# Causal attention block on one core: a power and a few idle products moved, and the mask of the narrow diagonal tiles added by TensorE

## Chip, cores and metric

One core of a Trainium2 chip runs the whole kernel. The metric is the device time of one execution in microseconds (us). The kernel before was timed three times.

## What is computed

One transformer layer over 8 sequences of 1024 tokens with 256 channels, 16 heads of 16 channels, in fp32:

```
mod = (silu(c) @ wmod) in six parts sa, ca, ga, sb, cb, gb
h = layernorm(x) * (1 + ca) + sa
scores = q @ k^T * 16 ** -0.5, the future keys masked; att = softmax(scores) @ v
x = x + ga * (att @ w_out + b_out)
h = layernorm(x) * (1 + cb) + sb
r = sigmoid(mix(h, mu_r) @ W_r); k = relu(mix(h, mu_k) @ W_k) ** 2
out = x + gb * r * (k @ W_v)
```

`mix(h, mu)` is `mu * h + (1 - mu) * (h shifted by one token)`. Full precision of the dense products comes from three products of split operands (hi by hi, hi by lo, lo by hi).

## The kernel before

Every engine has its program written out by hand; semaphores tie them. A sequence b is cut into four quarters s of four heads, a quarter into 12 steps t. In a quarter three things run side by side.

**Columns.** For the heads of quarter s, `score_columns` (L1246) makes scores with the keys on the partitions, in two PSUM banks `col_ps`. ScalarE takes the exponential into `weights` (`exps`, L823). In steps 0 to 3 and 8 to 11 the tile has the diagonal in it and GpSimd zeroes the future keys (`select`, L669). `values` (L1309) multiplies the weights of the step before with v. Steps 0 to 3 and 8 to 11 have 512, 384, 256 and 128 queries a head, steps 4 to 7 have 512.

**Rows.** The exponential needs the maximum of each query over its keys beforehand. So while quarter s runs its columns, `row_pair` (L1287) makes the scores of quarter s+1 with the queries on the partitions, in four banks `row_ps`, and VectorE reduces each bank to a maximum (`maximum`). A row unit is one bank: for query tile i, keys up to 512 or the rest. A diagonal unit ends at the diagonal. With up to 256 keys a unit holds two heads, otherwise one. A quarter has 40 units, handed out to steps by `PER_STEP`, two by two, those of even heads and odd heads on the two halves of the array's rows. The first two of a step are its early units, the others its late ones. In a diagonal unit `maximum` runs one fused add-and-max per head with `row_mask` (L1044, a CUSTOM_DVE instruction and one that reads its accumulator). In another unit it runs one TENSOR_REDUCE (L1048). A bank can be written again once its maximum has been taken (`row_bank`).

The narrow diagonal units are those of two heads: i = 0 (128 keys a head) early in step 0, i = 1 (256 keys) late in step 0, the second part of i = 4 (128) early in step 4, the second part of i = 5 (256) early in step 6. Each stands for a pair of banks: four pairs a quarter, 128 pairs in the run.

**Dense units.** Between them run the products of the next sequence (q, k, v and transposes, `front`) and of the sequence that has left attention (`back`: out, norm, recept, key, value, at steps 2, 6, 10, 11 and 13 of a quarter's own count, so that 12 to 15 fall into the next quarter). The recept and key products wait for `mix_lo` (L725), the value product for `k_lo` (L729), both made by GpSimd. In quarter 0 VectorE takes the layernorm sums of the next sequence (`layernorm_stats`, steps `STATS_STEPS`, L1082 and L1086), and GpSimd turns them into reciprocal deviations with a power (`rstd`, steps `RSTD_STEPS`, L655 to L660). ScalarE uses them in steps 2 and 3 of quarter 1. GpSimd's program in a step is: front, back, select, rstd, finish.

**Unused products.** `keep_load` (L1261) makes eight products of 512 columns into two `col_ps` banks that nobody reads, in quarters 2 and 3 at the start of step 3 and in quarters 1 and 3 at the columns of step 4. They first wait until the exponentials have left the banks.

TensorE's order in a step is: early rows, columns, values of the step before, then late rows and second columns (late rows first where a dense unit follows), dense units.

## Time and profile before

| | |
|---|---|
| median of 3 runs | 1496.95 us (1493.8 to 1501.97) |
| the profiled execution | 1493.7 us, its span 1492.0 us |
| mean granted TensorE clock | 0.961 of full speed |
| busy | TensorE 1339.4, its weight loads 759.3, VectorE 1153.5, ScalarE 958.3, GpSimd 666.9 us |

The profile comes from one execution. A row of the timeline gives the start, the duration of the merged group, the engine, the line, the operation and, in brackets, the idle time before it with what ended it. PE is TensorE's products, PEld its weight loads, DVE VectorE, ACT ScalarE, POOL GpSimd. Times in brackets are what a step of the chain waited; a matmul's duration holds its way through the array, so that the spacing of starts tells what a product takes from the stream.

### The profile page before, as it was taken

The numbers are of one execution on the slowest core, as the hardware profiler recorded it, in microseconds if no ns is written. First come the engines' busy times: TensorE is split into PE (matmuls) and PEld (weight loads), VectorE is DVE, ScalarE is ACT, GpSimd is POOL, SyncE is SP. The second block draws the span as 40 slices with busy tenths as digits, with TensorE's granted clock in tenths as the row PEclk, the third lists the DMA queues.
The fourth block names the chain that finished last, engine by engine and source line by source line (L and its number), as shares of the span: only waits on it lengthen the run. The fifth ranks groups of instructions, "written<-read, shape, count | busy, mean of one in ns | idle before, by whom it ended". The sixth has DMA issues, their size and how long they took to land.

```text
span 1492.0 us, 28255 instructions
## 1 busy us (share of the span) xinstructions
PE 1339.4 (90%) x9000; PEld 759.3 (51%) x9000; DVE 1153.5 (77%) x3627; ACT 958.3 (64%) x1916; POOL 666.9 (45%) x1042
## 2 busy tenths in 40 slices
PE   5799988999989999899999999899999999999855
PEld 4444444455644556555554556445555555544444
DVE  8788878877778778887788777787788777888234
ACT  2067666766668666667667666686666676666634
POOL 4023123544445444553445445454445535444554
PEclk9599999999999999999999999999999999999978
DMA  4322233212331224222332123312232222321100
GB/s 142 61 68 53 55 77 89 58 52 73 102 81 45 54 67 113 65 55 66 76 93 59 52 72 102 81 46 54 74 109 62 55 66 74 97 63 52 38 30 29
DMA packets 84133, 102.84 MB, mean 69 GB/s; under 512 B 20736, under 2 KB 49672, under 8 KB 83984
## 3 DMA queue, kind: packets, MB, share of 16 engines
q1 hardware_dynamic: 83408, 100.24, 25.4%
q8 instruction: 72, 1.18, 0.3%
q10 hardware_dynamic: 576, 0.79, 0.3%
q14 instruction: 77, 0.63, 0.1%
HBM read 31.74 MB, written 8.94 MB: 27 GB/s over the span
## 4 chain that ended last, share of the span: by engine, by line
PE 64%; ACT 12%; POOL 7%; issue 7%; DVE 6%; SPq 2%; DMA 2%; ACTq 0%; POOLq 0%; DVEq 0%
PE val_ps L1309 15%; PE col_ps L1246 14%; PE row_ps L1287 11%; ACT weights L823 7%; PE dense_ps L1347 5%; PE dense_ps L1319 4%; PE dense_ps L1321 3%; PE dense_ps L1320 3%; POOL weights L669 3%; PE dense_ps L1362 2%; PE dense_ps L1353 2%; SPq L498 2%; PE col_ps L1261 2%; PE dense_ps L1338 1%; ACT xn_c L867 1%
## 5 line engine op out<-in xcount | busy, mean ns | idle before, releaser
L823 ACT ACTIVATE weights<-col_ps 128x512 f32<-128x512 f32 (+2 forms) x1280 | 643.8, 556 | 285.5 <-PE col_ps L1246 270.1
L1044 DVE CUSTOM_DVE_ANT_0 row_ps<-row_ps,row_mask 128x128 f32<-128x128 f32 (+3 forms) x1024 | 477.2, 518 | 172.5 <-PE row_ps L1287 169.8
L669 POOL TENSOR_SCALAR_AFFINE_SELECT weights<-weights 128x256 f32<-128x256 f32 x512 | 211.3, 422 | 524.8 <-ACT weights L823 521.3
L1246 PE MATMUL col_ps<-q_stack,k_stack 64*128 64x512 f32 (+3 forms) x1536 | 394.1, 392 | 24.5 <-ACT weights L823 21.5
L1048 DVE TENSOR_REDUCE max_parts<-row_ps 128x1 f32<-128x512 f32 x512 | 328.1, 682 | 58.9 <-PE row_ps L1287 57.4
L1287 PE MATMUL row_ps<-k_stack,q_stack 62*128 62x512 f32 (+3 forms) x1536 | 328.4, 419 | 25.4 <-DVE max_parts L1048 10.9
L1309 PE MATMUL val_ps<-weights,v_ones 128*32 128x512 f32 (+3 forms) x3072 | 333.4, 506 | 18.1 <-POOL weights L669 9.2
L1246 PEld LDWEIGHTS col_ps<-q_stack,k_stack 64*128 64x128 f32 x1536 | 205.4, 187 | 209.0 <-ACT weights L823 191.5
L1287 PEld LDWEIGHTS row_ps<-k_stack,q_stack 62*128 62x128 f32 x1536 | 158.5, 190 | 226.4 <-DVE max_parts L1044 73.5
L1044 DVE DVE_READ_ACCUMULATOR2_ANT max_parts<- 128x1 f32 x1024 | 145.0, 142 | 0.0
L1309 PEld LDWEIGHTS val_ps<-weights,v_ones 128*32 128x32 f32 x3072 | 61.5, 108 | 105.2 <-issue 59.8
L725 POOL TENSOR_TENSOR mix_lo<-mixed,mix_hi 128x512 fp32r<-128x512 f32 x64 | 81.3, 1293 | 17.4 <-ACT mix_hi L916 15.2
L718 POOL TENSOR_TENSOR h_diff<-h 128x512 f32<-128x512 f32 x32 | 33.3, 1041 | 109.1 <-ACT h L887 108.9
L1148 DVE SCALAR_TENSOR_TENSOR mixed<-h_diff,mus,h 128x256 f32<-128x256 f32 x128 | 63.3, 535 | 10.2 <-POOL h_diff L718 10.2
L1319 PE MATMUL dense_ps<-h_hi,w_hi 128*128 128x512 f32 x124 | 55.5, 448 | 3.2 <-POOL h_lo L644 3.2
L1076 DVE STREAM_TRANSPOSE max_rows<-max_parts 32x32 f32<-32x32 f32 x256 | 51.3, 200 | 5.1 <-DVE max_parts L1070 0.3
L897 ACT ACTIVATE h_diff<-dense_ps 128x512 f32<-128x512 f32 x28 | 16.7, 598 | 57.1 <-PE dense_ps L1368 57.1
L1321 PE MATMUL dense_ps<-h_hi,w_lo 128*128 128x512 f32 x124 | 49.2, 397 | 0.0
L1320 PE MATMUL dense_ps<-h_lo,w_hi 128*128 128x512 f32 x124 | 49.0, 395 | 0.0
L894 ACT ACTIVATE mix_out<-dense_ps 128x512 f32<-128x512 f32 x28 | 16.8, 598 | 49.1 <-PE dense_ps L1353 49.1
L679 POOL TENSOR_TENSOR h_lo<-h_full,h_hi 128x512 fp32r<-128x512 f32 x28 | 35.9, 1280 | 26.7 <-DVE h_full L1108 26.7
L729 POOL TENSOR_TENSOR k_lo<-k_sq,k_hi 128x512 fp32r<-128x512 f32 x28 | 36.3, 1295 | 21.5 <-ACT k_hi L921 21.5
(196 smaller groups left out, 1946.0 us busy)
## 6 DMA issues: line engine op xcount, KB each, us to landing
q_stack<-q_part SPq DMA_DIRECT2D x384, 64.0 KB, 2.2
k_stack<-k_part SPq DMA_DIRECT2D x372, 64.0 KB, 2.2
xa<-in_x SPq DMA_DIRECT2D x9, 1024.0 KB, 6.4
att<-val_out SPq DMA_DIRECT2D x64, 128.0 KB
recips<-recip_rows SPq DMA_DIRECT2D x32, 256.0 KB
xq<-in_x SPq DMA_DIRECT2D x28, 256.0 KB, 3.2
out<-xq SPq DMA_DIRECT2D x28, 256.0 KB, 2.1
q_stack<-max_rows SPq DMA_DIRECT2D x128, 8.0 KB
```

The costliest lines, as they stand in the source:

```text
L669: nc.gpsimd.affine_select(out=w, in_=w, compare_op=ALU.is_ge, fill=0.0, base=0, pattern=[[0, 2], [1, P]], channel_multiplier=-1).then_inc( ...
L725: nc.gpsimd.tensor_tensor(mix_lo[:, m], mixed[:, m], mix_hi[:, m].bitcast(F32), ALU.subtract).then_inc(mix_lo_done, 1)
L823: nc.scalar.activation(weights[:, t % 2, heads[0]:heads[-1] + 1:2, 0:q1 - q0], col_ps[bank][:, 0:n * (q1 - q0)].rearrange("p (h q) -> p h ...
L1044: last = nc.vector.tensor_tensor_reduce(out=scores, in0=scores, in1=row_mask[:, HALF - width:HALF], scale=1.0, scalar=MASKED, op0=ALU.add, ...
L1048: last = nc.vector.reduce_max(dest, bank[:, 0:len(heads) * width].rearrange("p (h k) -> p h k", h=len(heads)), AX_X)
L1246: last = nc.tensor.matmul(col_ps[bank][:, i * (q1 - q0):(i + 1) * (q1 - q0)], stack_at(k_stack[s % 2], rows, heads[i], P * j, P * (j + 1)) ...
L1287: last = nc.tensor.matmul(banks[odd][:, n * width:(n + 1) * width], stack_at(q_stack[stack], rows, heads[n], P * i, P * (i + 1)), stack_at ...
L1309: last = nc.tensor.matmul(val_ps[32 * h:32 * h + 32, q0 - base:q1 - base], v_ones[:, j, G * s + h].rearrange("p d a -> p (d a)"), weights[ ...
L1319: nc.tensor.matmul(dst, a_hi(c), b_hi(c), start=(c == 0), stop=False)
L1320: nc.tensor.matmul(dst, a_hi(c), b_lo(c), start=False, stop=False)
L1321: last = nc.tensor.matmul(dst, a_lo(c), b_hi(c), start=False, stop=(c == KC - 1))
L1347: nc.tensor.matmul(dense[:, i, :], a_hi[:, c, P * i:P * (i + 1)], w(part, at, D)(c), start=(part is w_hi and i == 0 and c == 0), stop=Fals ...
```

## The change

Three things. (1) `RSTD_STEPS` goes from (0, 9) and (1, 0) to (0, 8) and (0, 11), and the last of `STATS_STEPS` from 11 to 9. (2) The unused products of quarters 2 and 3 at the start of step 3 go behind the values of step 3, ahead of its late rows, and take the banks of step 4, so that they wait for the exponentials of step 3. (3) In narrow diagonal units TensorE adds the mask: per head and half two products of `mask_ident` (64 rows by 128, bf16, an identity in two pieces) with `mask_fill` (bf16, -3e38 above the diagonal), 128 and 64 columns wide, accumulated onto the scores. VectorE then runs one TENSOR_REDUCE over both heads. Wide diagonal units (one head a bank) stay as they were. The constants are built by GpSimd at the start.

```
-LOAD_AT_START, LOAD_AT_COLUMNS, LOADS = ((2, 3), (3, 3)), ((1, 4), (3, 4)), 4
-SPLIT_STEP, STATS_STEPS, NORM_STEPS = 5, (5, 7, 8, 11), (2, 2, 3, 3)
-RSTD_STEPS = ((0, 9), (1, 0))
+LOAD_AT_ROWS, LOAD_AT_COLUMNS, LOADS = ((2, 3), (3, 3)), ((1, 4), (3, 4)), 4
+SPLIT_STEP, STATS_STEPS, NORM_STEPS = 5, (5, 7, 8, 9), (2, 2, 3, 3)
+RSTD_STEPS = ((0, 8), (0, 11))
...
 # maximum, VectorE
-                if k1 == P * (i + 1):
-                    for n in range(len(heads)):
-                        scores = bank[:, n * width:(n + 1) * width]
-                        last = nc.vector.tensor_tensor_reduce(...)
+                if k1 == P * (i + 1) and len(heads) == 1:
+                    scores = bank[:, 0:k1 - k0]
+                    last = nc.vector.tensor_tensor_reduce(...)
                 else:
                     last = nc.vector.reduce_max(...)
...
 # keep_load(b, s, t, after), TensorE
-                            pe.wait_ge(exp_done, exp_index(b, s, COL_FIRST[t] + odd) + (1 - ago))
+                            pe.wait_ge(exp_done, exp_index(b, s, COL_FIRST[t + after] + odd) + (1 - ago))
...
 # row_pair, TensorE
+                diagonal = k1 == P * (i + 1) and len(pair[0]) == 2
-                        end = n == len(heads) - 1
+                        end = n == len(heads) - 1 and not diagonal
...
+                for n in range(len(pair[0])) if diagonal else ():
+                    for a in range(2):
+                        for odd in range(2):
+                            rows = slice(ROW_TILE * odd, ROW_TILE * (odd + 1))
+                            end = n == len(pair[0]) - 1 and a == 1
+                            last = nc.tensor.matmul(banks[odd][:, (n + 1) * width - P + ROW_TILE * a:(n + 1) * width],
+                                                    mask_ident[rows, a, :], mask_fill[rows, a, ROW_TILE * a:P],
+                                                    start=False, stop=end, skip_group_check=True)
+                            if end:
+                                last.then_inc(rows_ready, 1)
...
 # body, TensorE
-                    if (s, t) in LOAD_AT_START and attends(kind):
-                        keep_load(b, s, t)
                     row_scores(b, s, early)
...
                     for c in cols[1:]:
                         score_columns(b, s, t, c)
+                    if (s, t) in LOAD_AT_ROWS and attends(kind):
+                        keep_load(b, s, t, 1)
                     if not dense_step:
                         row_scores(b, s, late)
```

GpSimd in quarters 0 and 1 of a sequence, from step 8 of quarter 0 (`h_diff` is made there) to step 1 of quarter 1. Before:

```order
L718 TENSOR_TENSOR h_diff<-h_0 128x512
L669 AFFINE_SELECT weights<-weights 128x2x128 x4
L655 TENSOR_SCALAR shift_a<-mv_a 128x4
L656 TENSOR_SCALAR var_a<-mv_a 128x4
L658 TENSOR_TENSOR rstd_a<-var_a,neg_half 128x4
L660 TENSOR_TENSOR shift_a<-shift_a,rstd_a 128x4
L725 TENSOR_TENSOR mix_lo<-mixed,mix_hi 128x512 x2
L669 AFFINE_SELECT weights<-weights 128x2x128 x6
L655 TENSOR_SCALAR shift_a<-mv_a 128x4
L656 TENSOR_SCALAR var_a<-mv_a 128x4
L658 TENSOR_TENSOR rstd_a<-var_a,neg_half 128x4
L660 TENSOR_TENSOR shift_a<-shift_a,rstd_a 128x4
```

`k_lo` follows. The same place in the change, from behind `h_diff` on:

```order
L682 AFFINE_SELECT weights<-weights 128x2x128 x2
L668 TENSOR_SCALAR shift_a<-mv_a 128x4
L669 TENSOR_SCALAR var_a<-mv_a 128x4
L671 TENSOR_TENSOR rstd_a<-var_a,neg_half 128x4
L673 TENSOR_TENSOR shift_a<-shift_a,rstd_a 128x4
L682 AFFINE_SELECT weights<-weights 128x2x128 x2
L738 TENSOR_TENSOR mix_lo<-mixed,mix_hi 128x512 x2
L682 AFFINE_SELECT weights<-weights 128x2x128 x4
L668 TENSOR_SCALAR shift_a<-mv_a 128x4
L669 TENSOR_SCALAR var_a<-mv_a 128x4
L671 TENSOR_TENSOR rstd_a<-var_a,neg_half 128x4
L673 TENSOR_TENSOR shift_a<-shift_a,rstd_a 128x4
```

The first power goes from ahead of `mix_lo` to ahead of the two selects of step 9, the second from behind the selects of the next quarter's step 0 to ahead of them; `k_lo` then follows those selects.

TensorE in quarter 2, steps 3 and 4, around the eight unused products (L1261 before, L1271 in the change). Before, from the unused products on:

```order
L1261 MATMUL col_ps1<-q_stack0,k_stack0 128x512
L1287 MATMUL row_ps0<-k_stack1,q_stack1 128x512
L1287 MATMUL row_ps1<-k_stack1,q_stack1 128x512
...
L1309 MATMUL val_ps<-weights,v_ones 32x256 x4
L1287 MATMUL row_ps2<-k_stack1,q_stack1 128x512
L1287 MATMUL row_ps3<-k_stack1,q_stack1 128x512
L1287 MATMUL row_ps0<-k_stack1,q_stack1 128x128
L1287 MATMUL row_ps1<-k_stack1,q_stack1 128x128
L1287 MATMUL row_ps0<-k_stack1,q_stack1 128x128
L1287 MATMUL row_ps1<-k_stack1,q_stack1 128x128
L1246 MATMUL col_ps0<-q_stack0,k_stack0 128x512
```

In the change, from the values of step 3 on:

```order
L1330 MATMUL val_ps<-weights,v_ones 32x256 x4
L1271 MATMUL col_ps0<-q_stack0,k_stack0 128x512
...
L1298 MATMUL row_ps2<-k_stack1,q_stack1 128x512
L1298 MATMUL row_ps3<-k_stack1,q_stack1 128x512
L1298 MATMUL row_ps0<-k_stack1,q_stack1 128x128
...
L1309 MATMUL row_ps0<-mask_fill,mask_ident 128x128
L1309 MATMUL row_ps1<-mask_fill,mask_ident 128x128
L1309 MATMUL row_ps0<-mask_fill,mask_ident 128x64
L1309 MATMUL row_ps1<-mask_fill,mask_ident 128x64
...
L1256 MATMUL col_ps0<-q_stack0,k_stack0 128x512
```

The first two row banks of step 3 are now written ahead of the unused products, and eight mask products stand between the narrow rows of step 4 and its columns.

## Rows read from the trace of the kernel before

**Rows 1.** The page: busy time of the engines, and the chain that ended last.

```profile
PE 1339.4 (90%) x9000; PEld 759.3 (51%) x9000; DVE 1153.5 (77%) x3627; ACT 958.3 (64%) x1916; POOL 666.9 (45%) x1042
...
PE 64%; ACT 12%; POOL 7%; issue 7%; DVE 6%; SPq 2%; DMA 2%; ACTq 0%; POOLq 0%; DVEq 0%
```

**Rows 2.** Waits: who waited for whom, us in total, times, longest.

```profile
PEld row_ps L1287 <- DVE max_parts L1044: 73.5, 124, 2.1
```

**Rows 3.** Timeline, quarter 0, step 10: start, duration, engine, line, work [idle].

```profile
605.97 1.05 POOL L658 TENSOR_TENSOR rstd_a<-var_a,neg_half 128x4 f32<-128x4 f32 x1 [0.15 <-POOL var_a L656]
606.02 0.39 PE L1347 MATMUL dense_ps<-w_hi,mix_hi 128*128 128x256 f32 x1
...
607.32 2.50 POOL L725 TENSOR_TENSOR mix_lo<-mixed,mix_hi 128x512 fp32r<-128x512 f32 x2
608.64 0.74 PE L1353 MATMUL dense_ps<-w_hi,mix_lo 128*128 128x256 f32 x4 [1.40 <-POOL mix_lo L725]
...
611.18 0.38 PE L1362 MATMUL dense_ps<-mix_hi,w_hi 128*128 128x256 f32 x1
```

**Rows 4.** Timeline, the same step of quarter 2 of the sequence before.

```profile
518.64 0.39 PE L1347 MATMUL dense_ps<-w_hi,mix_hi 128*128 128x256 f32 x1
...
521.79 0.38 PE L1362 MATMUL dense_ps<-mix_hi,w_hi 128*128 128x256 f32 x1
```

**Rows 5.** Timeline, quarter 1, step 1.

```profile
617.17 1.80 POOL L658 TENSOR_TENSOR rstd_a<-var_a,neg_half 128x4 f32<-128x4 f32 x1 [0.15 <-POOL var_a L656]
...
620.59 0.74 PE L1353 MATMUL dense_ps<-w_hi,k_lo 128*128 128x256 f32 x4 [0.85 <-POOL k_lo L729]
```

**Rows 6.** Windows: busy us of each engine, PEclk, DMA share, GB/s.

```profile
436.00:438.00 2.00, 2.00 (x11) 1.99 (x10) 1.59 (x7) 0.00 (x0) 0.00 (x0) 0.50 0.52 118
...
608.00:610.00 2.00, 1.34 (x10) 1.02 (x10) 0.17 (x1) 0.59 (x1) 2.00 (x3) 1.00 0.00 0
```

**Rows 7.** Timeline of TensorE: step 9 of quarter 0 to step 0 of quarter 1, twice.

```profile
427.38 1.08 PE L1287 MATMUL row_ps<-k_stack,q_stack 62*128 62x512 f32 x4
...
439.56 0.98 PE L1246 MATMUL col_ps<-q_stack,k_stack 64*128 64x512 f32 x2 [0.32 <-ACT weights L823]
...
603.55 1.08 PE L1287 MATMUL row_ps<-k_stack,q_stack 62*128 62x512 f32 x4
...
614.19 0.99 PE L1246 MATMUL col_ps<-q_stack,k_stack 64*128 64x512 f32 x2 [0.32 <-ACT weights L823]
```

**Rows 8.** Timeline, quarter 2, steps 3 and 4.

```profile
666.04 1.19 PE L1261 MATMUL col_ps<-q_stack,k_stack 62*128 62x512 f32 x8
...
668.11 0.68 DVE L1131 TENSOR_TENSOR xq<-xq,dense_ps 128x512 f32<-128x512 f32 x1
...
668.70 1.88 DVE L1048 TENSOR_REDUCE max_parts<-row_ps 128x1 f32<-128x512 f32 x3
...
669.44 0.43 PE L1287 MATMUL row_ps<-k_stack,q_stack 62*128 62x128 f32 x3 [0.75 <-DVE max_parts L1048]
...
670.09 1.09 ACT L823 ACTIVATE weights<-col_ps 128x512 f32<-128x512 f32 x2 [1.76 <-PE col_ps L1246]
```

**Rows 9.** Timeline, quarter 0, step 4: a narrow pair and what follows.

```profile
582.16 0.44 PE L1287 MATMUL row_ps<-k_stack,q_stack 62*128 62x128 f32 x4
...
582.44 0.44 PE L1246 MATMUL col_ps<-q_stack,k_stack 64*128 64x512 f32 x2
```

**Rows 10.** Timeline, quarter 3, step 6: columns behind a narrow pair.

```profile
718.86 0.99 PE L1246 MATMUL col_ps<-q_stack,k_stack 64*128 64x512 f32 x2 [0.45 <-ACT weights L823]
```

**Rows 11.** Groups by form: busy us, mean ns, idle before and its releaser.

```profile
L1048 DVE TENSOR_REDUCE max_parts<-row_ps 128x1 f32<-128x512 f32 x512 | 328.1, 682 | 58.9 <-PE row_ps L1287 57.4
...
L1044 DVE CUSTOM_DVE_ANT_0 row_ps<-row_ps,row_mask 128x256 f32<-128x256 f32 x256 | 102.2, 454 | 25.3 <-PE row_ps L1287 24.6
...
L1044 DVE CUSTOM_DVE_ANT_0 row_ps<-row_ps,row_mask 128x128 f32<-128x128 f32 x256 | 66.9, 321 | 13.8 <-PE row_ps L1287 12.3
```

More of the change, by code:

```diff
@@ L148, in build @@
         ident = sb("ident", [P, P])
+        mask_ident = sb("mask_ident", [P, 2, P], BF16)
+        mask_fill = sb("mask_fill", [P, 2, P], BF16)
         row_mask = sb("row_mask", [P, HALF], BF16)
@@ L619, in _ @@
             nc.gpsimd.memset(ident[:], 0.0)
+            nc.gpsimd.memset(mask_ident[:], 0.0)
+            nc.gpsimd.memset(mask_fill[:], 0.0)
             nc.gpsimd.memset(row_mask[:], 0.0)
@@ L626, in _ @@
                                     pattern=[[-1, P]], channel_multiplier=1).then_inc(consts_done, 1)
+            for odd in range(2):
+                pool.wait_ge(consts_done, odd + 1)
+                rows = slice(ROW_TILE * odd, ROW_TILE * (odd + 1))
+                nc.gpsimd.affine_select(out=mask_ident[rows], in_=mask_ident[rows], compare_op=ALU.not_equal, fill=1.0,
+                                        base=0, pattern=[[ROW_TILE, 2], [-1, P]], channel_multiplier=1)
+                nc.gpsimd.affine_select(out=mask_fill[rows], in_=mask_fill[rows], compare_op=ALU.is_ge,
+                                        fill=MASKED, base=0, pattern=[[ROW_TILE, 2], [-1, P]],
+                                        channel_multiplier=1).then_inc(consts_done, 1)
+            pool.wait_ge(consts_done, 3)
             nc.gpsimd.affine_select(out=row_mask[:, HALF - P:HALF], in_=row_mask[:, HALF - P:HALF], compare_op=ALU.is_ge,
@@ L630, in _ @@
                                     ).then_inc(consts_done, 1)
-            pool.wait_ge(consts_done, 2)
+            pool.wait_ge(consts_done, 4)
             def open_first():
@@ L1038, in maximum @@
                 dest = max_parts[half][:, col:col + 4 * len(heads) - 3:4].bitcast(F32)
-                width = k1 - k0
-                if k1 == P * (i + 1):
-                    for n in range(len(heads)):
-                        scores = bank[:, n * width:(n + 1) * width]
-                        last = nc.vector.tensor_tensor_reduce(
-                            out=scores, in0=scores, in1=row_mask[:, HALF - width:HALF], scale=1.0, scalar=MASKED,
-                            op0=ALU.add, op1=ALU.max, accum_out=dest[:, n:n + 1])
+                if k1 == P * (i + 1) and len(heads) == 1:
+                    scores = bank[:, 0:k1 - k0]
+                    last = nc.vector.tensor_tensor_reduce(
+                        out=scores, in0=scores, in1=row_mask[:, HALF - (k1 - k0):HALF], scale=1.0, scalar=MASKED,
+                        op0=ALU.add, op1=ALU.max, accum_out=dest)
                 else:
-                    last = nc.vector.reduce_max(dest, bank[:, 0:len(heads) * width].rearrange(
+                    last = nc.vector.reduce_max(dest, bank[:, 0:len(heads) * (k1 - k0)].rearrange(
                         "p (h k) -> p h k", h=len(heads)), AX_X)
@@ L1251, in score_columns, with keep_load @@
                             last.then_inc(cols_ready, 1)
-            def keep_load(b, s, t):
+            def keep_load(b, s, t, after):
                 for n in range(LOADS):
@@ L1292, in row_pair @@
                             last.then_inc(rows_ready, 1)
+                for n in range(len(pair[0])) if diagonal else ():
+                    for a in range(2):
+                        for odd in range(2):
+                            rows = slice(ROW_TILE * odd, ROW_TILE * (odd + 1))
+                            end = n == len(pair[0]) - 1 and a == 1
[4 more added lines that the diff above has]
+                                last.then_inc(rows_ready, 1)
             def values(b, s, t):
@@ L1380, in open_first @@
             def open_first():
-                pe.wait_ge(consts_done, 2)
+                pe.wait_ge(consts_done, 4)
                 for k in range(4):
@@ L1467, in body @@
                     unit = front_unit(b, kind, s, t)
-                    if (s, t) in LOAD_AT_START and attends(kind):
-                        keep_load(b, s, t)
                     row_scores(b, s, early)
                     if (s, t) in LOAD_AT_COLUMNS and attends(kind):
-                        keep_load(b, s, t)
+                        keep_load(b, s, t, 0)
                     for c in cols[:1]:
```

## The prediction, written before the change was run

> **What bounds the kernel now.** I read the page's busy line and its chain first. TensorE is busy 90% of the span and holds 64% of the chain that ended last; ScalarE, GpSimd and VectorE hold 12, 7 and 6% [rows 1]. So no engine is the bound all through: TensorE's stream is, broken by short waits for the three others. What a part of this change is worth is therefore what it adds to that stream where nothing is waited for behind it, less the waits it takes out. Next come the waits: TensorE's weight loads for row scores stood 73.5 us before maxima of line 1044 [rows 2]. Then the timeline of one sequence tells where the waits sit. A sequence takes about 174 us, and its pattern repeats.
>
> Three places matter. In quarter 0, step 10, GpSimd's power (1.05 us, with two small operations ahead and one behind it) sits between the selects of step 9 and `mix_lo`, and the recept product waits 1.40 us for `mix_lo` [rows 3]. In quarter 1, step 1, the second power takes 1.80 us ahead of `k_lo`, and the value product waits 0.85 us [rows 5]. In quarters 2 and 3 the unused products take TensorE from 666.04 on, so that the rows of step 3 and their maxima start late, with an add of 0.68 us in VectorE's program between them; the narrow pair of step 4 then waits 0.75 us for a free bank, and ScalarE has by then stood 1.76 us for its next columns [rows 8]. A fourth thing is the clock. In five of the six sequences that have the wait of rows 3, TensorE's granted clock falls from 1.00 to 0.50 (from 2.4 to 1.2 GHz) right behind it and stays there for some 3.4 us; in the sixth it stays at 1.00 [rows 6].
>
> **The change, part by part.**
>
> *The first power, (0, 9) to (0, 8).* The power now stands behind the selects of step 8, where GpSimd waits for ScalarE anyway, and `mix_lo` starts once step 9 is selected. The same step in another quarter, which has no such power, shows what is left: from the first recept product to the first key product 521.79 - 518.64 = 3.15 us [rows 4] against 611.18 - 606.02 = 5.16 us [rows 3]. The difference, 2.0 us, is on the path. Six sequences have both the power and a recept product here: -12.0 us. What could be late next is the first select of step 9, by about half a microsecond. The second select of that step, for which the values really wait, comes over a microsecond later, so I price this at nothing and keep +0.6 a sequence as its bound.
>
> *The second power, (1, 0) to (0, 11), and the sums of step 11 to step 9.* The power now fills the gap ahead of the next quarter's first exponentials. `k_lo` starts when `k_hi` is there: -0.85 us in six sequences, -5.1 us [rows 5]. The two sums and their two aggregates stand about 1.1 us longer in VectorE's program in step 9 and as much less in step 11; the maxima behind them have two free banks of slack. Nothing.
>
> *The clock.* What a fall costs is told by two sequences of the same work. From the late rows of step 9 to the first waiting columns of quarter 1 it is 439.56 - 427.38 = 12.18 us with the fall and 614.19 - 603.55 = 10.64 us without [rows 7]: 1.5 us. If the idle stretch ahead of it goes, I expect the five falls to go: -7.5 us. Bounds: 0, and -7.5 with a few us more from the other falls in the trace.
>
> *The unused products of step 3.* Moved behind the values, they no longer hold up the two rows of step 3. VectorE has its first bank 1.0 us earlier, does the add and the second bank while TensorE works through the unused products, and the narrow pair finds both banks free. TensorE's count of work is the same. What goes is the wait: 0.75 us by its bracket, and about 0.16 more, because the bracket begins at the end of the product before, whose way through the array is no time of the stream (in rows 9 a group of 0.44 us takes 0.28 of it): 0.91 us. ScalarE is idle before the columns that follow, so nothing else takes its place: 2 quarters by 8 sequences by 0.91 = -14.6 us. The new wait for the exponentials of step 3 ends about when the values do; bound +0.2 each.
>
> *The masks on TensorE.* 128 pairs get 8 products each, 1024 in all, with as many weight loads. No bf16 product with 64 rows is in the trace. The nearest row is a narrow pair without masks: 4 products of 128 columns take the stream 582.44 - 582.16 = 0.28 us, in two rounds in which the two halves of the array work together [rows 9]. Eight products are four rounds, so 0.56 us is the upper end. The lower end is pure streaming, two rounds of 128 columns and two of 64 at 2.4 GHz: 384 / 2400 = 0.16 us. I take 0.38, somewhat nearer the row, since there too the rounds are longer than their columns (0.14 for 0.053). The Trainium skill, "TensorE: Matmul & The Clock Gate", section "Weight-path perf modes", says that weights of 128 columns in another type than FP32 are loaded faster, measured about twice as fast. By that a round would be about half as long, a pair 0.28 us and the sum 8 us lower; no row here shows such a load.
>
> What of it lies on the path: the pair of step 0 (i = 0) stands ahead of the columns that ScalarE's run of exponentials waits for, in all four quarters. The late pair of step 0 is followed in quarters 1 to 3 by columns that wait 0.32 us for ScalarE [rows 7], so it is mostly hidden there and half in quarter 0. The pair of step 4 is on the path in quarters 2 and 3 [rows 8] and in quarter 0, where the columns start at once behind it [rows 9]; in quarter 1 ScalarE is busy normalising the next sequence. The pair of step 6 is hidden in quarters 1 and 3, where the columns wait 0.45 us [rows 10], and counts in quarters 0 and 2, among dense products. That is 4 + 0.5 + 3 + 2 = 9.5 of 16 a sequence, 76 in all: 76 by 0.38 = +28.9 us; 12.2 and 42.6 at the ends.
>
> *The maxima on VectorE.* Two fused operations of 128 columns (321 ns) and two of 256 (454 ns) become reduces of 256 and 512 columns; the latter takes 682 ns, and 128 columns are worth 454 - 321 = 133 ns, so the former about 416 [rows 11]. That is 642 to 416 and 908 to 682, 0.23 us less a bank by durations, for 256 banks 58 of the 1153.5 busy us [rows 1]. VectorE sees the pair of banks later by the mask, though, and its waits at narrow units are for TensorE. The waits of rows 2 are largely behind wide units. I take nothing; bounds 0 and -10.
>
> *GpSimd at the start* builds two more constants, some 2 us, while it would wait for the sums of the first sequence. Nothing.
>
> **The sum**: -12.0 - 5.1 - 7.5 - 14.6 + 28.9 = -10.3 us. Against the profiled execution's 1493.7 that is 1483.4; the median of the runs shown stands 3.25 above that execution, so I forecast **1487 us** for the median. Half a per cent, 7.5 us, is about what a measurement of this kernel can tell from no change: below 1489.5 is faster, above 1504.4 slower.
>
> **The rivals.**
>
> *The masks are nearly free* (0.16 a pair): -10.3 - 16.7 = -27.0, that is 1470 us for the median. For it: half of the products are 64 wide and the weights are half as many bytes. Against it: rounds of 128 columns take over twice their streaming in every row I have. The page named above stands on this side.
>
> *The gains are partly given back.* The 39.2 us of gains rest on four places, and what follows each has its own pace. If the clock falls elsewhere in each sequence instead (the wait of rows 3 may be the occasion and not the cause: one sequence of six has the wait and no fall), its 7.5 us do not come: 1494 us. If ScalarE's exponentials also take half of what the unused products give, 7.3 more are lost: 1501 us. Both are no change that can be told. Against it: ScalarE stood idle 1.76 us at rows 8, and rows 4 show the short form of the step in this very kernel.
>
> *The masks stay on the path everywhere*, slower. If the pairs I call hidden only push the wait on (TensorE is 90% busy, and the late pair of step 0 also delays the rows that VectorE's queue waits for), all 128 count; at the upper 0.56 that is 71.7 - 39.2 = +32.5, 1529 us. It decides from 39.2 / 128 = 0.31 us a pair if all lie on the path, or from 0.52 us at my 76. For it: the price per round measured here is exactly the upper end. Against it: the waits of 0.32 and 0.45 us stand in the rows behind those pairs.
>
> *The first power only moves its wait*: it holds the selects of step 9 and the values behind them, +0.6 by 6 in place of part of the gain, 1491 us.
>
> **How the numbers follow.** The forecast case gets 0.40 (1477 to 1497), about two thirds of it below 1489.5; free masks 0.20; gains given back 0.22; masks everywhere 0.13; the moved wait 0.05. Faster: 0.27 + 0.20 + 0.02 and a part of the third case, 0.05, = 0.54. Slower: 0.13 and 0.02 from the ends of the others = 0.15. The rest is 0.31. The range goes from 1466 to 1505: it has the free masks at its lower end and the given-back gains at its upper, and leaves out most of the slower case.
>
> **What the profile of the changed kernel would show.** Right: recept's `mix_lo` products without idle time in quarter 0, the value product without idle in quarter 1; no 0.75 us before the narrow pair of step 4; no clock of 0.50 behind step 10 of quarter 0; 1024 more products at a spacing by which eight take 0.3 to 0.45 us; VectorE's busy time down by 50 us or more. Wrong: eight mask products at over 0.5 us, longer waits of ScalarE for columns in steps 0 and 4, falls of the clock at new places, or the wait for `select` grown ahead of the values of step 9.

## The result, and the profile after

The changed kernel takes 1476.92 us (median of 4 runs, 1474.35 to 1478.59) against 1495.38 us for the kernel before, timed beside it (median of 4). The ratio is 0.987, with a 95% interval of 0.9831 to 0.9908: faster by about 1.3%. The forecast was 1487 us, 10 us faster, with a range of 1466 to 1505; the gain measured is 18.5 us. The profiled execution took 1476.08 us, its span is 1474.4 us; before it was 1492.0.

The page of the changed kernel, its busy line and its chain:

```profile
PE 1349.9 (92%) x10024; PEld 780.7 (53%) x10024; DVE 1117.6 (76%) x2859; ACT 958.0 (65%) x1916; POOL 670.3 (45%) x1048
...
PE 68%; ACT 10%; issue 6%; POOL 5%; DVE 4%; SPq 4%; DMA 2%; ACTq 0%; POOLq 0%; DVEq 0%
```

Against [rows 1], TensorE is busy 10.5 us longer in a span 17.6 us shorter, and GpSimd's share of the chain goes from 7 to 5%.

The timeline around step 10 of quarter 0 and the start of quarter 1 (start, duration, engine, line, work, idle before in brackets); it answers to [rows 3] and [rows 5]:

```profile
596.93 1.04 POOL L671 TENSOR_TENSOR rstd_a<-var_a,neg_half 128x4 f32<-128x4 f32 x1 [0.15 <-POOL var_a L669]
...
599.85 2.53 POOL L738 TENSOR_TENSOR mix_lo<-mixed,mix_hi 128x512 fp32r<-128x512 f32 x2
...
600.59 0.38 PE L1368 MATMUL dense_ps<-w_hi,mix_hi 128*128 128x256 f32 x1
...
601.65 0.64 PE L1374 MATMUL dense_ps<-w_hi,mix_lo 128*128 128x256 f32 x4
...
603.74 0.39 PE L1383 MATMUL dense_ps<-mix_hi,w_hi 128*128 128x256 f32 x1
...
605.02 1.04 POOL L671 TENSOR_TENSOR rstd_a<-var_a,neg_half 128x4 f32<-128x4 f32 x1 [0.15 <-POOL var_a L669]
...
605.34 0.44 PE L1298 MATMUL row_ps<-k_stack,q_stack 62*128 62x128 f32 x4
...
605.62 0.35 PE L1309 MATMUL row_ps<-mask_fill,mask_ident 64*128 64x128 bf16 x8
...
605.80 0.48 PE L1256 MATMUL col_ps<-q_stack,k_stack 64*128 64x512 f32 x2
...
606.96 0.98 PE L1256 MATMUL col_ps<-q_stack,k_stack 64*128 64x512 f32 x2 [0.32 <-ACT weights L836]
```

`mix_lo` now starts 0.74 us ahead of the first recept product, and the products with `mix_lo` have no idle time ahead. From the first recept product to the first key product it is 603.74 - 600.59 = 3.15 us, the length that [rows 4] promised, in place of 5.16 [rows 3]. The value product of quarter 1, which waited 0.85 us for `k_lo` in [rows 5], follows its neighbour at the pace of the others:

```profile
612.21 0.29 PE L1368 MATMUL dense_ps<-w_lo,k_hi 128*128 128x256 f32 x1
612.34 0.64 PE L1374 MATMUL dense_ps<-w_hi,k_lo 128*128 128x256 f32 x4
```

Eight mask products take the stream 605.80 - 605.62 = 0.18 us (0.19 in other places). The columns behind the late pair still wait 0.32 us for ScalarE, as in [rows 7].

TensorE in step 3 of quarter 2, where the unused products (L1271) moved behind the first rows and the values:

```profile
659.62 0.50 PE L1298 MATMUL row_ps<-k_stack,q_stack 62*128 62x512 f32 x2
...
660.80 1.21 PE L1271 MATMUL col_ps<-q_stack,k_stack 62*128 62x512 f32 x7
...
662.08 0.39 PE L1298 MATMUL row_ps<-k_stack,q_stack 62*128 62x512 f32 x3
```

Nothing waits ahead of the narrow rows; the 0.75 us of [rows 8] are gone.

Windows of the changed kernel, columns as in [rows 6]: step 10 of quarter 0, and then step 10 of quarter 1.

```profile
600.00:602.00 2.00, 2.00 (x19) 1.41 (x12) 1.85 (x7) 1.19 (x3) 2.00 (x2) 1.00 0.03 8
602.00:604.00 2.00, 1.73 (x19) 0.99 (x18) 2.00 (x7) 1.26 (x3) 1.64 (x5) 1.00 0.00 0
...
644.00:646.00 2.00, 2.00 (x11) 1.68 (x12) 0.00 (x0) 0.53 (x1) 0.78 (x1) 0.50 0.00 0
```

The clock stays at full speed where it fell in [rows 6]. It falls to half (1.2 GHz) at another place, 43 us later, in three of six sequences. The row there:

```profile
642.69 0.40 PE L1368 MATMUL dense_ps<-w_hi,mix_hi 128*128 128x256 f32 x1 [1.56 <-DVE h_full L1118]
```

**Where the time went.** The values of steps 0 and 4 are the only products 128 columns wide of their line, eight groups a sequence. Their starts cut each sequence into eight places. "Steady" below is the shortest of the six full sequences at each place, summed and taken six times; "falls" is what the six took beyond that. Most of it lies at a granted clock of 0.50, but not all: the first place of the second sequence is 1.5 us longer than in the others in both kernels, at a clock of 1.00, and it stands in this column too. In us of each profiled span:

| kernel | steady | falls | first sequence | last | rest | span |
|---|---|---|---|---|---|---|
| before | 1032.9 | 13.2 | 216.7 | 162.9 | 66.3 | 1492.0 |
| the change | 1017.4 | 6.8 | 221.1 | 161.9 | 67.2 | 1474.4 |

The difference of 17.6 us is 15.5 steady and 6.4 of falls, less 4.4 lost in the first sequence; the last sequence and the rest give 0.1 together. How the 15.5 divide, the experiments tell.

The 4.4 us sit in two places of the first sequence: steps 0 to 4 of quarter 2 take 13.35 us in place of 10.24, and those of quarter 3 take 14.41 in place of 12.34, while the other places together got 0.8 shorter. In both, the rows of step 3 wait for the DMA that brings `k_stack`, and the clock falls behind the wait. These rows of the changed kernel, in quarter 2 and in quarter 3, and a window of quarter 2:

```profile
153.63 0.50 PE L1298 MATMUL row_ps<-k_stack,q_stack 62*128 62x512 f32 x2 [1.58 <-DMA k_stack<-k_part]
192.08 0.56 PE L1298 MATMUL row_ps<-k_stack,q_stack 62*128 62x512 f32 x2 [1.52 <-DMA k_stack<-k_part]
...
156.00:158.00 2.00, 2.00 (x21) 2.00 (x18) 0.66 (x2) 0.00 (x0) 0.00 (x0) 0.50 0.00 0
```

Before, the unused products stood ahead of these rows. In quarter 2 TensorE does not wait for this DMA then, in quarter 3 it waits 0.56 us, and the clock is at 1.00 at both places. So part (2) of the change can lay this wait bare, which the prediction did not look at. How much of the 4.4 us is its work is not shown: in three executions of one and the same code (e4, e9 and e10 below) the wait is 0.48 us and none, 0.48 and none, none and 1.45, and in e3, whose unused products stay where they were, it is 0.70 and 0.67.

### The profile page after: what moved, and what is told of

It reads as the page before. It is cut to its first block, busy times and chain, and to the rows that moved or that the text cites. A ratio compares the mean times of both kernels' runs of the same rounds, so it can differ in the third digit from the quotient of the medians.

```text
span 1474.4 us, 29545 instructions
## 1 busy us (share of the span) xinstructions
PE 1349.9 (92%) x10024; PEld 780.7 (53%) x10024; DVE 1117.6 (76%) x2859; ACT 958.0 (65%) x1916; POOL 670.3 (45%) x1048
## 4 chain that ended last, share of the span: by engine, by line
PE 68%; ACT 10%; issue 6%; POOL 5%; DVE 4%; SPq 4%; DMA 2%; ACTq 0%; POOLq 0%; DVEq 0%
PE val_ps L1330 16%; PE col_ps L1256 15%; PE row_ps L1298 11%; ACT weights L836 7%; PE dense_ps L1368 5%; PE dense_ps L1340 4%; SPq L500 3%; PE dense_ps L1342 3%; PE dense_ps L1341 3%; POOL weights L682 3%; PE col_ps L1271 2%; PE dense_ps L1374 2%; PE dense_ps L1383 2%; PE dense_ps L1359 2%; ACT xn_c L880 1%
## 5 line engine op out<-in xcount | busy, mean ns | idle before, releaser
L1058 DVE TENSOR_REDUCE max_parts<-row_ps 128x1 f32<-128x512 f32 (+2 forms) x768 | 457.3, 638 | 130.8 <-PE row_ps L1298 69.3
L1054 DVE CUSTOM_DVE_ANT_0 row_ps<-row_ps,row_mask 128x384 f32<-128x384 f32 (+1 forms) x512 | 309.3, 648 | 117.2 <-PE row_ps L1298 115.6
L1298 PE MATMUL row_ps<-k_stack,q_stack 62*128 62x512 f32 (+3 forms) x1536 | 329.4, 419 | 15.8 <-ACT v_ones L822 7.5
L1330 PE MATMUL val_ps<-weights,v_ones 128*32 128x512 f32 (+3 forms) x3072 | 329.4, 501 | 14.4 <-POOL weights L682 4.9
L1298 PEld LDWEIGHTS row_ps<-k_stack,q_stack 62*128 62x128 f32 x1536 | 163.9, 190 | 205.0 <-DVE max_parts L1058 94.1
L1054 DVE DVE_READ_ACCUMULATOR2_ANT max_parts<- 128x1 f32 x512 | 72.5, 142 | 0.0
L1158 DVE SCALAR_TENSOR_TENSOR mixed<-h_diff,mus,h 128x256 f32<-128x256 f32 x128 | 63.2, 534 | 10.5 <-POOL h_diff L731 10.5
L1309 PE MATMUL row_ps<-mask_fill,mask_ident 64*128 64x128 bf16 (+1 forms) x1024 | 54.4, 210 | 0.0
L742 POOL TENSOR_TENSOR k_lo<-k_sq,k_hi 128x512 fp32r<-128x512 f32 x28 | 40.1, 1431 | 24.5 <-ACT k_hi L934 24.5
```

Source lines behind the costliest of these rows:

```text
L1054: last = nc.vector.tensor_tensor_reduce(out=scores, in0=scores, in1=row_mask[:, HALF - (k1 - k0):HALF], scale=1.0, scalar=MASKED, op0=ALU. ...
L1058: last = nc.vector.reduce_max(dest, bank[:, 0:len(heads) * (k1 - k0)].rearrange("p (h k) -> p h k", h=len(heads)), AX_X)
L1298: last = nc.tensor.matmul(banks[odd][:, n * width:(n + 1) * width], stack_at(q_stack[stack], rows, heads[n], P * i, P * (i + 1)), stack_at ...
L1330: last = nc.tensor.matmul(val_ps[32 * h:32 * h + 32, q0 - base:q1 - base], v_ones[:, j, G * s + h].rearrange("p d a -> p (d a)"), weights[ ...
```

## The experiments

Each was timed in three rounds beside the kernel before. Ratios are to it, with 95% intervals.

### One part at a time

**e1_power**: the kernel before with the steps of the powers and sums alone.

```
-SPLIT_STEP, STATS_STEPS, NORM_STEPS = 5, (5, 7, 8, 11), (2, 2, 3, 3)
-RSTD_STEPS = ((0, 9), (1, 0))
+SPLIT_STEP, STATS_STEPS, NORM_STEPS = 5, (5, 7, 8, 9), (2, 2, 3, 3)
+RSTD_STEPS = ((0, 8), (0, 11))
```

> The kernel before with only the power and the sums of layernorm moved (steps (0, 8) and (0, 11), sums at 9). Theory A (the waits for mix_lo and k_lo were on the path, by the same stretch of the changed kernel 1.55 us and about 1.1 us a sequence in six sequences, and the five falls of the clock behind the first wait cost 1.5 us each): 16 less, 7.5 of them for the clock, if no new falls come; 12 to 16 less with falls elsewhere. Theory B (the gain came from the unused products and the masks, the waits for GpSimd only move on to ScalarE): under 5 us less. The recept product's wait for mix_lo in quarter 0 is gone in both.

Measured: 1474.51 us, ratio 0.9856 (0.9835 to 0.9878), 21.9 us less than before and more than the 12 to 16 expected. The place with the first power went from 30.63 to 28.64 us, 2.0 less; the one with the second from 15.36 to 14.22, 1.13 less (both are middle values of the sequences without a fall; by the shortest ones, as in the table above, they are 2.08 and 1.12, 19.2 us over six sequences). The falls did not go: before, five were in step 10 of quarter 0, now all six sequences have one in step 10 of quarter 1. Two windows of e1_power there:

```profile
468.00:470.00 2.00, 0.51 (x2) 0.51 (x3) 1.55 (x4) 1.39 (x3) 2.00 (x4) 0.86 0.02 4
470.00:472.00 2.00, 2.00 (x11) 2.00 (x10) 0.11 (x2) 0.00 (x0) 1.60 (x2) 0.50 0.00 0
```

TensorE is busy 0.51 of 2 us and then at half clock. In the kernel before the same idle stretch is there, and no fall follows it (its row, in the sequence of [rows 3], and the window behind it, at a clock of 1.00):

```profile
650.83 0.39 PE L1347 MATMUL dense_ps<-w_hi,mix_hi 128*128 128x256 f32 x1 [1.55 <-DVE h_full L1108]
...
652.00:654.00 2.00, 2.00 (x22) 1.34 (x21) 1.01 (x3) 1.26 (x3) 1.23 (x2) 1.00 0.00 0
```

So with the first idle stretch gone, the falls came at the next one.

**e2_unused**: the kernel before with the unused products of step 3 behind the values.

```
-                    if (s, t) in LOAD_AT_START and attends(kind):
-                        keep_load(b, s, t)
                     row_scores(b, s, early)
...
                         score_columns(b, s, t, c)
+                    if (s, t) in LOAD_AT_ROWS and attends(kind):
+                        keep_load(b, s, t, 1)
```

> The kernel before with only the unused products of quarters 2 and 3, step 3, moved behind the values. Theory A (the 0.75 us wait of the narrow pair in step 4 was on the path): each half quarter from step 0 to step 4 of quarters 2 and 3 is 0.8 to 0.9 us shorter, 13 to 15 us in all. Rival (ScalarE or VectorE take the place of the wait): under 5 us less.

Measured: 1483.98 us, ratio 0.9916 (0.9897 to 0.9936). The two places got 0.81 and 0.84 us shorter and the two behind them 0.1 each, 11.0 us steady. The median is 12.5 us below the kernel before, just under the 13 to 15 expected.

**e3_masks**: the change without the other two parts.

```
-RSTD_STEPS = ((0, 8), (0, 11))
+RSTD_STEPS = ((0, 9), (1, 0))
...
-                    if (s, t) in LOAD_AT_ROWS and attends(kind):
-                        keep_load(b, s, t, 1)
```

> The kernel before with only the masks of the narrow diagonal units added by TensorE and one reduce on VectorE. Theory A (eight mask products take 0.19 us of TensorE's stream by the changed kernel's starts, and 9 to 10 of 16 pairs a sequence lie on the path; VectorE's relief gives nothing): 9 to 15 us more than before. Theory C (VectorE's shorter maxima free the row banks sooner and pay for the products): no change, or up to 8 us less.

Measured: 1507.53 us, ratio 1.0062 (1.004 to 1.0083), **slower**. The median is 11.1 us above the kernel before, as theory A had it (9 to 15), and theory C is out. The steady time rose by 14.4 us (1047.3), while the falls took 5.6 in place of 13.2.

**e4_nomask**: the change with the maxima and masks as before.

```
-                if k1 == P * (i + 1) and len(heads) == 1:
+                if k1 == P * (i + 1):
...
-                for n in range(len(pair[0])) if diagonal else ():
```

> The changed kernel with its masks back on VectorE, that is the power and the unused products moved and nothing else. Theory A (the masks cost 9 to 15 us): 9 to 15 us faster than the changed kernel, near 1465 us, about 30 less than before. Theory C (the masks give something in this surrounding, where TensorE waits less elsewhere): at or above the changed kernel's 1477 us. A third outcome, near 1477: they cost as much as they give.

Measured: 1459.44 us (1453.9 to 1460.51), ratio 0.9742 (0.9717 to 0.9768). It beats both kernels; its median is 17.5 us below the changed kernel's, a little more than the 9 to 15 expected. Steady it is 1002.6, which is 30.3 less than before and 14.8 less than the change. The parts add up: -19.2 for e1 (with the place that always has a fall there taken at its length without one, 27.1 us), -11.0 for e2 and +14.4 for e3 are -15.8, against -15.5 for the change as a whole.

### The price of a mask, and VectorE's relief

**e5_double**: the change with every mask product issued twice (and a third of the fill, -1e38, so that the sum stays in range).

```
-                        for odd in range(2):
+                        for odd in (0, 1, 0, 1):
```

> The changed kernel with every mask product made twice (16 instead of 8 a pair; -1e38 instead of -3e38, so that the sum stays finite). VectorE's work is as in the changed kernel, so this doubles the price of the products alone. Theory A (the products' stream time lies on the path at some 12 of 16 pairs a sequence): by starts a group takes 0.38 us instead of 0.19, a sequence without a fall of the clock is 2.3 us longer, the run 15 to 20 us longer than the changed kernel's 1477. Theory C (it was the late release of VectorE, not TensorE's time, that cost): less than half of that.

Measured: 1493.39 us, ratio 0.9959 (0.9941 to 0.9978; the kernel before beside it 1499.88), 16.5 us above the changed kernel's median, as theory A had it. Sixteen products, and then the next columns, in its timeline:

```profile
568.84 0.52 PE L1310 MATMUL row_ps<-mask_fill,mask_ident 64*128 64x128 bf16 x16
569.20 0.47 PE L1256 MATMUL col_ps<-q_stack,k_stack 64*128 64x512 f32 x2
```

That is 0.36 us, 0.17 to 0.18 more than eight. The sequence grew by 2.05 us, as much as some 11.5 of its 16 pairs; the first set of masks adds 2.41 by the places below and 2.47 by the steady sums (from e4 to the change), some 13 pairs at 0.19. By place, e4 to the change, and then the doubling (middle values of the sequences without a fall):

| from values to values | change - e4 | e5 - change | pairs I called on the path |
|---|---|---|---|
| quarter 0, step 0 to 4 | 0.30 | 0.34 | 1.5 |
| step 4 to quarter 1, step 0 | 0.46 | 0.36 | 2 |
| quarter 1, step 0 to 4 | 0.19 | 0.26 | 0 |
| step 4 to quarter 2, step 0 | 0.24 | 0.16 | 1 |
| quarter 2, step 0 to 4 | 0.20 | 0.19 | 1 |
| step 4 to quarter 3, step 0 | 0.55 | 0.35 | 2 |
| quarter 3, step 0 to 4 | 0.21 | 0.18 | 1 |
| step 4 to the next sequence | 0.26 | 0.21 | 1 |

At 0.19 a pair my count is too low by some three pairs. A pair more lies on the path in quarter 1, steps 0 to 4, where I called both hidden; ahead of quarter 3 it is 0.17 us more than two pairs; the rest is spread over the other places.

**e6_reduce_only**: e4 with the narrow diagonal units reduced without any mask.

```
-                if k1 == P * (i + 1):
+                if k1 == P * (i + 1) and len(heads) == 1:
```

> The power and the unused products moved, and VectorE reduces the narrow diagonal units with one reduce and no mask at all: the mask of the narrow tiles is left out, so the maximum may be that of a future key. It is the relief of VectorE without TensorE's products. Theory A (the relief gives nothing): the same as the version with neither, 1459 us, within 3 us. Theory C (the relief is worth something that the products hide): 5 to 15 us faster than that.

Measured: 1459.88 us, ratio 0.9747 (0.97 to 0.9794), as e4, and the same middle length at all eight places, within 0.02 us. VectorE's busy time of e6 on its page:

```profile
PE 1330.5 (91%) x9000; PEld 754.0 (52%) x9000; DVE 1115.1 (77%) x2859; ACT 957.7 (66%) x1916; POOL 666.0 (46%) x1042
```

It is 37 us below e4's 1152.4, and nothing of it reaches the end. The masks on TensorE cost their price at some 12 or 13 of 16 pairs, and the relief that they give VectorE buys nothing.

### What the unused products cost

**e7_noload3** and **e8_noload**: e4 without the unused products of step 3 of quarters 2 and 3, and without any.

```
-LOAD_AT_ROWS, LOAD_AT_COLUMNS, LOADS = ((2, 3), (3, 3)), ((1, 4), (3, 4)), 4
+LOAD_AT_ROWS, LOAD_AT_COLUMNS, LOADS = (), ((1, 4), (3, 4)), 4
```

(e8: both empty.)

> The power moved, masks on VectorE, and the unused products of quarters 2 and 3 at step 3 taken out altogether (those at step 4 stay). Theory D (behind the values they still take about 0.9 us of TensorE's path each): half quarters 0 to 4 of quarters 2 and 3 get shorter by 0.5 to 0.9, 8 to 14 us less than 1459. Rival (the clock falls where they stood, 1.5 to 3 us a fall): falls in most sequences at step 3 to 5 of these quarters, 10 to 25 us more than 1459.

> As the run before, with the unused products at step 4 of quarters 1 and 3 out too, so that no unused product is left. Theory D: another 5 to 12 us less. Rival (the clock): more falls than in the run before, 10 to 30 us more than 1459 us.

Measured: e7 1465.2 us, ratio 0.9781 (0.9744 to 0.9818); e8 1466.88, ratio 0.9794 (0.9764 to 0.9825). Both medians are above e4's, but their intervals overlap with it: they are not faster, and not clearly slower. Neither the 8 to 14 us less of theory D nor the 10 us more of the rival came. Without the products of step 3 the two places are 0.10 us shorter each, and the two behind them 0.12 and 0.10 longer: in the new place 128 products, some 1 us a group on TensorE, were hidden. Falls took 16.4 and 18.1 us in place of e4's 10.0. Four of e7's five falls in quarters 2 and 3 stand some 3 us behind the values of step 0, where e4 has three, and not where the products were. In e8's steady time there is a gain (996.9 against 1002.6) that the falls take back. It comes from quarter 3, where steps 0 to 4 are 1.03 us shorter a sequence; in quarter 1 they are 0.94 shorter, but the place behind is 0.90 longer. So the unused products of step 4 do cost TensorE time in quarter 3.

### Where the clock falls

**e9_t_early** and **e10_t_eight** were to move the dense units of the transposed kind, the cause of the idle stretch in step 10 of quarter 1. The edit was not in the files: both ran the code of e4.

> Both powers and the unused products as in the change, masks on VectorE (the kernel that gave 1459.4 us), and beside that the four steps at which the dense units of the transposed kind are worked are 3, 4, 5 and 7 in place of 3, 5, 7 and 9, so that no such unit is worked in the step before step 10. Theory (clock): TensorE's idle stretch of about 1.5 us in step 10 of quarter 1, while dense_ps is freed late, is what the falls of the clock follow; with it gone position q1 step 4 to q2 step 0 shortens by 1 to 1.5 us a sequence, plus 1.45 us for each fall that is there, and the run is 1440 to 1450 us. Rival: the dense units of steps 4, 5 and 7 wait for the bank instead, or the falls go to another idle stretch, and the run is 1459 us or more.

> As the run before, but the four steps are 3, 5, 7 and 8 in place of 3, 5, 7 and 9: only the last unit moves, by one step. Theory (clock): the idle stretch in step 10 of quarter 1 shrinks, its falls go, and the run is 1443 to 1455 us. Rival: the unit of step 8 keeps ScalarE and GpSimd as late as that of step 9 did, or the falls move on, and the run is 1459 us or more.

Measured: 1461.75 us, ratio 0.9748 (0.9713 to 0.9783), and 1457.87 us, ratio 0.9743 (0.9709 to 0.9777). They tell nothing of the theory. As repeats of e4 they show how far the same code scatters: 12 runs from 1453.5 to 1464.6 us, and in the profiled executions 10.0, 12.2 and 12.7 us of falls with a steady time of 1002.5 to 1003.0.

**e11_t_early** and **e12_t_eight**: the edit proper (e12: 3, 5, 7, 8).

```
-V_EARLY, V_STEPS, QK_STEPS, T_STEPS = (7, 9), (0, 3), (4, 5, 7, 8), (3, 5, 7, 9)
+V_EARLY, V_STEPS, QK_STEPS, T_STEPS = (7, 9), (0, 3), (4, 5, 7, 8), (3, 4, 5, 7)
```

> The two runs before this were to move the dense units of the transposed kind, but their files were e4's, unedited: they are repeats of it (1461.8 and 1457.9 us). Here the four steps at which these units are worked in quarter 1 are 3, 4, 5 and 7 in place of 3, 5, 7 and 9, and nothing else differs from the kernel with both powers and the unused products moved and the masks on VectorE. Theory (clock): TensorE's idle stretch of 1.55 us in step 10 of quarter 1, while dense_ps is freed late, goes, and with it the falls of the clock that follow it; the position q1 step 4 to q2 step 0 shortens by 1 to 1.5 us a sequence and the run is 1440 to 1450 us. Rival: the dense units of steps 4, 5 and 7 wait for the bank instead, or the falls go to another place, and the run is 1458 us or more.

> As the run beside it, but the four steps are 3, 5, 7 and 8: only the last unit moves, by one step. Theory (clock): the idle stretch in step 10 of quarter 1 shrinks and its falls go, 1443 to 1455 us. Rival: the unit of step 8 keeps ScalarE and GpSimd as late as that of step 9 did, or the falls move on, and the run is 1458 us or more.

Measured: e11 **1452.22 us** (1451.38 to 1458.31), ratio 0.9704 (0.9688 to 0.972), the fastest of all; e12 1459.55, ratio 0.9752 (0.9733 to 0.977). Step 10 of quarter 1 in e11:

```profile
636.02 0.85 PE L1309 MATMUL val_ps<-weights,v_ones 128*32 128x384 f32 x8
...
636.81 0.38 PE L1347 MATMUL dense_ps<-w_hi,mix_hi 128*128 128x256 f32 x1
```

The idle stretch is gone, the place takes 26.2 us in all six sequences where e4 took 27.1 without a fall and 28.6 with one, and none of the six falls there. But four of the six now fall behind the start of quarter 2, where e4 had one in six. Two windows of e11, and its timeline ahead of them:

```profile
476.00:478.00 2.00, 1.81 (x13) 1.15 (x17) 1.41 (x7) 2.00 (x5) 0.81 (x2) 0.93 0.44 104
478.00:480.00 2.00, 2.00 (x10) 0.44 (x4) 1.26 (x6) 1.34 (x4) 1.33 (x2) 0.50 0.44 98
```

```profile
475.44 0.99 PE L1246 MATMUL col_ps<-q_stack,k_stack 64*128 64x512 f32 x2 [0.33 <-ACT weights L823]
475.93 0.91 PE L1287 MATMUL row_ps<-k_stack,q_stack 62*128 62x256 f32 x6
476.63 0.93 PE L1246 MATMUL col_ps<-q_stack,k_stack 64*128 64x384 f32 x2
477.70 1.93 PE L1309 MATMUL val_ps<-weights,v_ones 128*32 128x512 f32 x8
```

In the 18 us ahead of this fall no idle stretch of TensorE is over 0.33 us. It costs 1.0 us. Both theories had a part: the steady time fell by 5.0 us (997.7), the falls by only 2 (8.1). e11 came out between the 1440 to 1450 of the one and the 1458 of the other. (The profiled execution is its slowest, 1458.31 us; the other three took 1451.38 to 1452.91.)

In e12 the idle of 1.56 us is gone too, but the place is no shorter (27.14 us); the wait has moved ahead in the same step:

```profile
632.67 0.50 PE L1287 MATMUL row_ps<-k_stack,q_stack 62*128 62x512 f32 x1 [1.04 <-DVE max_parts L1048]
```

In its profiled execution the granted clock is 1.00 all through the six sequences: there is no fall at all, and the 2.9 us of its column lie at full clock, most of them in the first place of the second sequence. That execution took 1456.2 us, the median is 1459.55, still e4's. One profiled execution's falls are no measure of a kernel.

## Why the prediction was right

The direction (faster) and the range held, and the median of 1476.92 us came 10 below the forecast of 1487: the gain is nearly twice the one forecast. By its own steps:

| term | predicted, us a sequence | measured, us a sequence | by |
|---|---|---|---|
| first power | -2.0 | -1.99 | e1 |
| second power | -0.85 | -1.13 | e1 |
| clock | -1.25 (five falls of 1.5 in six) | -1.07 | the two profiles |
| unused products | -1.82 | -1.84 | e2 |
| masks | +3.61 (9.5 pairs of 0.38) | +2.40 to +2.47 | e3, e4 |
| VectorE's relief | 0 | 0 | e6 |

The measured column is for the six full sequences. Over these, the steady terms of the prediction make -1.06 and the measured ones -2.58 a sequence.

*The powers.* The short form of the step in another quarter [rows 4] gave the first one exactly. The second was read from its bracket, 0.85 us; it gave 1.13. The bracket begins at the end of the product before, as the prediction said of the unused products, and the same correction here (0.16) would have made it 1.01. Sums in step 9 and the selects behind the power cost nothing that the places show.

*The unused products.* 0.75 in the bracket and 0.16 for the product's way through the array was 0.91 a quarter. The places gave 0.81 and 0.84, and 0.1 in each place behind: 0.92.

*The masks.* **This is the step that was wrong in its size**: "I take 0.38, somewhat nearer the row". The pair costs 0.19 us, below the 0.3 to 0.45 that the prediction looked for in the changed profile, near the lower end of pure streaming (0.16), and not the 0.56 of the narrow rows. One thing in which the two kinds differ shows in the weight loads, grouped by form (busy us, mean ns, idle before):

```profile
L1298 PEld LDWEIGHTS row_ps<-k_stack,q_stack 62*128 62x128 f32 x1536 | 163.9, 190 | 205.0 <-DVE max_parts L1058 94.1 <-issue 41.5 <-DVE max_parts L1054 31.0
...
L1309 PEld LDWEIGHTS row_ps<-mask_fill,mask_ident 64*128 64x128 bf16 x1024 | 34.9, 98 | 2.4
```

A load of 128 columns takes 98 ns in bf16 and 190 in FP32. The Trainium skill, "TensorE: Matmul & The Clock Gate", section "Weight-path perf modes", says that weights of 128 columns in another type than FP32 load about twice as fast: the trace agrees. The price that the prediction worked out from it, 0.28 a pair, was nearer than mine, and the measured one is lower still. That the faster loads are what makes the masks cheap is my reading: no run changes the type of the weights alone. The rival of nearly free masks had the price nearly right (0.16) and the time too low (1470), mostly because it kept the count of 76 pairs: some 13 pairs a sequence at 0.19 are 7 us more over eight sequences. The first sequence took 4.4 us more.

The count of pairs on the path was too low: 9.5 a sequence predicted, some 13 by e4 against the change and 11.5 by the doubling. So the price was twice what it measured and the count a quarter too low, and the second error hid part of the first. 76 by 0.19 would have been 14.4 us in place of 28.9, and the forecast 1472; the 2.4 a sequence that was measured is 19.2 over eight, and with it the forecast would have been 1477, the median measured. That it fits so closely is partly luck: the 4.4 us lost in the first sequence and the second power's surplus, 1.7, are in neither.

*VectorE.* A reduce of 256 columns takes 416 ns, as worked out from [rows 11]; its groups after the change:

```profile
L1058 DVE TENSOR_REDUCE max_parts<-row_ps 128x2 f32<-128x512 f32 x128 | 83.4, 678 | 45.4 <-PE row_ps L1309 45.4
...
L1058 DVE TENSOR_REDUCE max_parts<-row_ps 128x2 f32<-128x256 f32 x128 | 48.5, 416 | 14.0 <-PE row_ps L1309 13.8
```

The busy time fell by 35.9 us, though, and not by 50 or more: the fused operations overlap, each starting before the one ahead ends, so that their durations overstate them (in the kernel before, those of 128 columns at 614.06, 614.30 and 614.55 start 0.25 us apart and last 0.33 each). That nothing of it counts was right (e6). TensorE's waits for maxima came to 135.1 us before (the 73.5 of [rows 2] and 61.6 for the reduces) and to 125.1 in the change, now mostly for the reduces:

```profile
PEld row_ps L1298 <- DVE max_parts L1058: 94.1, 155, 1.5
...
PEld row_ps L1298 <- DVE max_parts L1054: 31.0, 57, 0.8
```

*The clock.* The number came out near, the reasoning did not. "If the idle stretch ahead of it goes, I expect the five falls to go": they did at that place, and e1 got six at the next idle stretch. Falls at new places were among the prediction's own signs of being wrong, and they came. That the falls are fewer in the change (three of six) cannot be put down to the powers. Over the kernels, those with mask products on TensorE have 5.6 to 9.0 us of falls in the profiled execution, those without 2.9 (e12, no fall in it) to 13.2, those with fewer unused products 16.4 and 18.1. Work on TensorE and falls go opposite ways in most of them, but e12 speaks against a simple rule, and the spread within the same code is 2.7 us. This stays open. The first sequence takes from 215.7 to 221.4 us, in kernels with masks and without; in the change it goes with the waits for the DMA of `k_stack` and the falls behind them, in the other kernels the cause was not looked for.

## What to carry to other kernels

Where the stream of TensorE is the bound, work moved to it from an engine that is off the path costs its price wherever TensorE does not wait anyway: here 1.2%, hidden under two good edits; try each part alone before keeping the sum. Read a wait's worth from the same step without the wait, not from its bracket. Price a product by its own kind, type and weight load together, and not by the nearest shape in another type. Before moving work that stands ahead of a transfer's user, ask what wait it covers.

## What the runs showed of the hardware

- Eight bf16 products with 64 rows, two halves of the array side by side, take 0.19 us of the stream, sixteen 0.36; their weight loads take 98 ns against 190 in FP32.
- A fall of TensorE's granted clock from 2.4 to 1.2 GHz mostly costs 1.0 to 1.5 us here. It can follow an idle stretch of 1.4 to 1.6 us, but the same stretch also stands without a fall (the row at 650.83 of the kernel before), and a fall also comes with no idle stretch over 0.33 us in the 18 us ahead (e11).
- One execution has no fall in its six full sequences (e12), others of nearly the same code and median have six or seven (e4, e9).
- Taking the occasion of falls away mostly moved them: from step 10 of quarter 0 to step 10 of quarter 1 (e1, six of six), and from there to the start of quarter 2 (e11, four of six).
- Unused products behind the values of step 3 are hidden (0.1 us each way, e7), and the two kernels that leave some or all of them out were not faster than e4.
